# Routing of two mixture-of-experts layers: token table ahead of the pass tables, and one of four place one-hots on ScalarE

## The reference, cut to what matters

```python
def _moe_forward(x, gate_w, wi_gate, wi_up, wo):      # layer 2; N = 2048, E = 8, 512 hidden
    capacity = max(int(N / E * CAPACITY_FACTOR), 1)   # 320
    router_probs = jax.nn.softmax(x_flat @ gate_w.T, axis=-1)
    top_k_probs, top_k_idx = jax.lax.top_k(router_probs, 2)
    top_k_probs = top_k_probs / jnp.sum(top_k_probs, axis=-1, keepdims=True)
    for k in range(2):
        eid = top_k_idx[:, k]
        onehot = (eid[:, None] == experts[None, :]).astype(jnp.int32)
        pos = (cumulative count of onehot)[token, eid] - 1
        disp = zeros(E, capacity, D).at[eid, pos].add(x_flat where pos < capacity)
        expert_out = (silu(disp @ wi_gate) * (disp @ wi_up)) @ wo
        out = out + top_k_probs[:, k] * expert_out[eid, pos]
# layer 3: the same top 2 of 8, without a capacity, h = gelu(x @ w1), out += weight * (h @ w2)
```

## Time and profile before

| | |
|---|---|
| median of 3 runs | 1176.15 us (1174.04 to 1177.28) |
| the profiled execution | 1177.07 us, its span 1175.5 us |
| routing of layer 2, from the router's first product to the first pass | 764.8 to 799.1 us |
| passes of layer 2 | 799.1 to about 909 us |
| routing of layer 3 | 1037.0 to 1071.6 us |
| passes of layer 3 | 1071.6 to about 1150 us |
| busy shares | PE 79%, DVE 72%, ACT 53%, POOL 44% |

### The profile page before, as it was taken

One profiled execution on the slowest core, in us unless ns is written; L12 is line 12 of the kernel. 1 busy time (PEld: TensorE's weight loads), 2 busy tenths in 40 slices (PEclk: granted clock), 3 DMA queues, 4 the chain that ended last, 5 costly groups with the idle time before them and its releaser, 6 DMA issues. The chain is left out here.

```text
span 1175.5 us, 18522 instructions
## 1 busy us (share of the span) xinstructions
PE 928.4 (79%) x5579; PEld 567.1 (48%) x5579; DVE 851.6 (72%) x1652; ACT 626.8 (53%) x1352; POOL 520.9 (44%) x527
## 2 busy tenths in 40 slices
PE   5988799999667856578888888868999296767992
PEld 3523345444445542223223322348999155756982
DVE  6887999999999377878887885184544568985333
ACT  3487798897243443236676667624553393232432
POOL 2056898899501323201111111125653466235773
PEclk9978999999877997669999999858999587867996
DMA  9000000000000301411110010061110200001113
...
DMA packets 28014, 46.29 MB, mean 39 GB/s; under 512 B 8720, under 2 KB 16408, under 8 KB 26896
## 3 DMA queue, kind: packets, MB, share of 16 engines
...
q0 software_dynamic: 4096, 8.35, 2.4%
...
## 5 line engine op out<-in xcount | busy, mean ns | idle before, releaser
L2106 DVE TENSOR_REDUCE sb_l_mxp<-ps 128x2 f32<-128x1024 f32 (+3 forms) x152 | 171.3, 1163 | 40.3 <-PE ps L1919 39.2
L1048 POOL TENSOR_TENSOR sb_gs<-sb_hs,sb_xp 128x512 f32<-128x512 f32 x128 | 162.4, 1296 | 23.9 <-DVE sb_hs L854 12.3
L2049 ACT ACTIVATE sb_l_pT<-ps 128x512 f32<-128x512 f32 (+3 forms) x256 | 111.4, 521 | 75.9 <-PE ps L1974 74.8
L680 PE MATMUL ps<-sb_gs,sb_ident 128*128 128x512 f32 x256 | 131.9, 606 | 0.2
L3042 PE MATMUL ps<-sb_hT,sb_f_shared 128*128 x936 | 121.5, 281 | 1.6 <-ACT sb_hT L3073 1.6
L3042 PEld LDWEIGHTS ps<-sb_hT,sb_f_shared 128*128 128x128 f32 x936 | 113.9, 197 | 2.8 <-issue 2.3
L1974 PE MATMUL ps<-sb_l_qk 51*128 51x512 bf16 (+3 forms) x384 | 88.5, 333 | 18.2 <-ACT sb_l_pT L2049 8.0
L3081 ACT ACTIVATE sb_f_hid<-ps 128x512 f32<-128x512 f32 x78 | 46.6, 597 | 78.6 <-PE ps L3042 78.6
L3140 POOL DMA_INDIRECT moe_y<-sb_f_rows,sb_f_rowi x64 | 64.1, 1001 | 52.9 <-DVE sb_f_rows L3112 41.0
L951 ACT ACTIVATE sb_dA<-sb_dt,sb_negA 128x512 f32<-128x512 f32 x109 | 77.7, 713 | 10.6 <-DVE sb_hs L854 9.8
L3051 PE MATMUL ps<-sb_sw_f_out,sb_f_hid 128*128 x624 | 82.5, 276 | 0.6 <-DVE sb_f_hid L3101 0.6
...
## 6 DMA issues: line engine op xcount, KB each, us to landing
sb_sw_f_in<-w_f_in SPq DMA_DIRECT2D x2, 2048.0 KB, 10.1
...
```

The costliest lines, as they stand in the source:

```text
L680: pe.matmul(ps[:, 4 + e * CPB + hf, :], ident[:], gs[:, p % SL, :], start=False, stop=n == DS - 1).then_inc(acc, 1)
L1048: gp.tensor_tensor(gs[:, q % SL, :], hs[:, q % SL, :], cs[:, k % 2, hf * CH:(hf + 1) * CH], ALU.mult).then_inc(times_c, 1)
L2049: ac.activation(pT[e % 3][:, h, 0:width], ps[:, bank[n_bank], 0:width], ACT.Exp, scale=L2_SCALE).then_inc(exped, 1)
L2106: dv.tensor_reduce(dst, src, AX_X, ALU.max).then_inc(max_out, 1)
```

## The change

Six edits, each in both layers:

1. The one-hots of the experts, `oh`, are written in the order of memory (experts outside, tiles inside), not across it.
2. Two roundings that were an addition and a subtraction in two instructions are one instruction each. The offsets `off` come ahead of `in_blk`, and a second copy of a quarter of them, `off_late`, in 32 bits.
3. VectorE makes three of the four pieces of `at_off`. The fourth (second choice, second half of the tiles) is made by ScalarE: eight Squares of (offset minus index) and one Relu of 1 minus that.
4. `vector_passes` is cut in two. `vector_edges` (the steps on 8 experts) stays behind `at_off`; the rest stands behind `tok_i`. The token table is read with three instructions straight from PSUM.
5. The transposes of chunk 0 back to rows stand behind the ranks with the other three chunks, as do their copies on ScalarE.
6. In the first pass TensorE's transposes of block 1 stand behind the first two of its hidden products.

```diff
@@ -2753,8 +2754,8 @@
             for k in range(2):
-                dv.tensor_tensor(oh[:, k].rearrange("p e t -> p t e"), iota[:].unsqueeze(1).to_broadcast([P, NT, NE]),
-                                 idx[:, :, k].unsqueeze(2).to_broadcast([P, NT, NE]), ALU.is_equal).then_inc(rt_ohb, 1)
+                dv.tensor_tensor(oh[:, k], iota[:].unsqueeze(2).to_broadcast([P, NE, NT]),
+                                 idx[:, :, k].unsqueeze(1).to_broadcast([P, NE, NT]), ALU.is_equal).then_inc(rt_ohb, 1)
             dv.wait_ge(rt_ohb, 3 * nth + 2)
@@ -2799,23 +2800,25 @@
-        def vector_passes():
-            wide = [P, NPASS, NE - 1]
+        def vector_edges():
...
             dv.wait_ge(*v_step.now())
-            dv.tensor_scalar(edge[:], edge[:], ROUND, None, ALU.add).then_inc(*v_step.up())
-            dv.wait_ge(*v_step.now())
-            dv.tensor_scalar(edge[:], edge[:], ROUND, None, ALU.subtract).then_inc(*v_step.up())
+            dv.tensor_scalar(edge[:], edge[:], ROUND, ROUND, ALU.add, ALU.subtract).then_inc(*v_step.up())
             dv.wait_ge(*v_step.now())
...
             dv.tensor_tensor_scan(ends[:], ones[:], ends[:], 0.0, ALU.mult, ALU.add).then_inc(*v_step.up())
-            dv.wait_ge(*v_step.now())
+            at_ends.append(v_step.now())
+        def vector_passes():
+            wide = [P, NPASS, NE - 1]
+            dv.wait_ge(*at_ends[0])
             dv.tensor_tensor(past_end[:], ends[:, 0:NE - 1].unsqueeze(1).to_broadcast(wide),
@@ -2868,48 +2871,51 @@
             dv.wait_ge(*v_step.now())
-            dv.tensor_scalar(sblk[:], sblk[:], ROUND, None, ALU.add).then_inc(*v_step.up())
+            dv.tensor_scalar(sblkb[:], sblk[:], ROUND, ROUND, ALU.add, ALU.subtract).then_inc(*v_step.up())
+            dv.tensor_scalar(sblk[:], sblk[:], ROUND, ROUND, ALU.add, ALU.subtract).then_inc(*v_step.up())
             dv.wait_ge(*v_step.now())
-            dv.tensor_scalar(sblkb[:], sblk[:], ROUND, None, ALU.subtract).then_inc(*v_step.up())
-            dv.tensor_scalar(sblk[:], sblk[:], ROUND, None, ALU.subtract).then_inc(*v_step.up())
-            dv.wait_ge(*v_step.now())
+            dv.scalar_tensor_tensor(off[:], sblk[:], -float(P), slot[:], ALU.mult, ALU.add).then_inc(*v_step.up())
+            at_off_ready = v_step.now()
+            dv.scalar_tensor_tensor(off_late[:], sblk[:, 1, HT:], -float(P), slot[:, 1, HT:], ALU.mult,
+                                    ALU.add).then_inc(rt_at, 1)
             for k in range(2):
...
                                  sblkb[:, k].unsqueeze(2).to_broadcast([P, NT, NSLOT]), ALU.is_equal).then_inc(rt_at, 1)
-            dv.scalar_tensor_tensor(off[:], sblk[:], -float(P), slot[:], ALU.mult, ALU.add).then_inc(*v_step.up())
-            dv.wait_ge(*v_step.now())
+            dv.wait_ge(*at_off_ready)
             for k in range(2):
-                for hf in range(2):
+                for hf in range(2 - k):
                     t0 = hf * HT
...
                                      ALU.is_equal).then_inc(rt_hot, 1)
-            vector_passes()
-            lo, hi = ids[:, 0], ids[:, 1]
+            vector_edges()
+            lo, tables = ids[:, 0], ps[:, 5, 0:2 * NSLOT].rearrange("p (a b) -> p a b", a=2)
+            hi = tables[:, 1]
             dv.wait_ge(rt_mm, r0 + MM_TABLE)
-            dv.tensor_copy(ids[:].rearrange("p a b -> p (a b)"), ps[:, 5, 0:2 * NSLOT]).then_inc(*v_step.up())
-            dv.wait_ge(*v_step.now())
-            dv.scalar_tensor_tensor(lo, lo, float(NT), hi, ALU.mult, ALU.add).then_inc(*v_step.up())
-            at_lo = v_step.now()
+            dv.tensor_copy(lo, tables[:, 0]).then_inc(*v_step.up())
             dv.tensor_scalar(tmp[:], hi, float(NT) + 0.5, float(-NT), ALU.is_gt, ALU.mult).then_inc(*v_step.up())
...
             at_row = v_step.now()
+            dv.wait_ge(*at_tmp)
+            dv.scalar_tensor_tensor(lo, lo, float(NT), hi, ALU.mult, ALU.add).then_inc(*v_step.up())
+            at_lo = v_step.now()
             dv.wait_ge(*at_lo)
             dv.tensor_scalar(tok[:], lo, -1.0, 0.0, ALU.add, ALU.max).then_inc(*v_step.up())
-            dv.wait_ge(*at_tmp)
             dv.wait_ge(*v_step.now())
...
             dv.scalar_tensor_tensor(row[:], tmp[:], float(-(NTOK - NT) // NT), row[:], ALU.mult, ALU.add).then_inc(*v_step.up())
-            dv.wait_ge(*v_step.now())
+            at_row = v_step.now()
+            vector_passes()
+            dv.wait_ge(*at_row)
             dv.scalar_tensor_tensor(row_i[:], lo, -1.0, row[:], ALU.add, ALU.add).then_inc(rt_tables, 1)
...
             for k in range(2):
-                gp.wait_ge(rt_at, 2 * nth + k + 1)
+                gp.wait_ge(rt_at, 3 * nth + k + 2)
                 gp.tensor_tensor(at_blk[:, k, :, 1, :], in_blk[:, k],
@@ -2939,7 +2945,6 @@
             routed(1)
-            back_to_rows(0)
             turned(3)
@@ -2949,13 +2954,16 @@
                       start=True, stop=True).then_inc(rt_mm, 1)
-            for c in range(1, NCH):
+            for c in range(NCH):
                 back_to_rows(c)
             for k in range(2):
-                pe.wait_ge(rt_lo, 2 * nth + k + 1)
+                pe.wait_ge(rt_lo, 3 * nth + k + 1)
                 pe.wait_ge(rt_hi, 2 * nth + k + 1)
                 for hf in range(2):
-                    pe.wait_ge(rt_hot, 4 * nth + 2 * k + hf + 1)
+                    if k + hf < 2:
+                        pe.wait_ge(rt_hot, 3 * nth + 2 * k + hf + 1)
+                    else:
+                        pe.wait_ge(rt_lo, 3 * (nth + 1))
                     for t in range(hf * HT, (hf + 1) * HT):
@@ -2969,16 +2977,20 @@
                 modulate_chunk(l, 1, mod_nth, c)
-                if c == NCH - 2:
-                    rows_evacuated(0)
-            for c in range(1, NCH):
+            for c in range(NCH):
                 rows_evacuated(c)
...
             for k in range(2):
-                ac.wait_ge(rt_at, 2 * nth + k + 1)
+                ac.wait_ge(rt_at, 3 * nth + k + 2)
                 ac.activation(at_blk[:, k, :, 0, :], in_blk[:, k], ACT.Copy, scale=w["c_f2_ids"][:, 2 * NT:2 * NT + 1]).then_inc(rt_lo, 1)
+            apart = hid[:, 0:2, :].rearrange("p z (t n) -> p (z t) n", n=P)
+            for t in range(HT):
+                i = ac.activation(apart[:, t, :], w["c_f2_iota"][:], ACT.Square, scale=-1.0, bias=off_late[:, t:t + 1])
+            i.then_inc(*a_step.up())
+            ac.wait_ge(*a_step.now())
+            ac.activation(at_off[:, 1, HT:, :], apart, ACT.Relu, scale=-1.0, bias=ones[:, 0:1]).then_inc(rt_lo, 1)
@@ -3026,11 +3038,15 @@
         def tensor_step(s):
-            for k in turns(s):
-                gathered(pe, k)
-                past_block(pe, s_x, k - 2)
-                pe.transpose(ps[:, TURN_BANK[k % 2], 0:P], in_q[:, k % QBUF, 0:D], ident[:]).then_inc(s_tr, 1)
+            def turn_blocks():
+                for k in turns(s):
+                    gathered(pe, k)
+                    past_block(pe, s_x, k - 2)
+                    pe.transpose(ps[:, TURN_BANK[k % 2], 0:P], in_q[:, k % QBUF, 0:D], ident[:]).then_inc(s_tr, 1)
             i = s + 1
+            if i != 0:
+                turn_blocks()
             if inside(i):
@@ -3041,6 +3057,8 @@
                                       start=True, stop=True)
+                        if i == 0 and n == 0 and f == FT // 2 - 1:
+                            turn_blocks()
                 m.then_inc(s_up, 1)
```

5 lines of the change are left out of this document (3 added, 2 removed).

## The result

| | before | after |
|---|---|---|
| median | 1176.72 us (1174.04 to 1178.35, 4 runs) | 1162.61 us (1160.65 to 1164.20, 4 runs) |
| ratio | | 0.986, interval 0.982 to 0.990 |
| profiled execution | 1177.07 us | 1160.65 us |

The kernel is 14.1 us faster.

The account below looks back on a forecast made before the run. Passes taken as bound by their start, so time saved in routing reaches the end: 4.6 us in layer 2 plus 4.1 in layer 3, 8.7 in all, median 1167.5 us (chance 0.59), range 1164 to 1171.5.

Parts of the forecast that it names:

- the clock: TensorE's clock around the first passes: 0.5 us lost per layer; bounds 1.9 us gained or 1.8 lost.
- Gelu's table load: Layer 3's first pass: the 1.28 us load ends at T + 8.9, first outputs at T + 10.1, gain 0.45 us.
- Expert one-hots: Routing, both layers: two instructions take 0.6 us in place of 1.23, gain 0.6 us per layer, bounds 0 and 0.9.
- Chunk 0: Its transposes leave the routing chain: 0.7 us gained in layer 3, 0 in layer 2.
- Offsets and GpSimd: Moving `off` ahead of GpSimd's multiplications gains 0.2 us, not 0.85, since the next two-input VectorE instruction waits instead.
- ScalarE's piece: Squares and Relu take 3.7 us, ending before VectorE's third piece in layer 2, after it in layer 3 (1061.3 against 1060.5).
- Rival A: ScalarE's piece comes 1 to 2 us later and bounds; T later by 1.3 us per layer, 1170.1 us; chance 0.17.
- rival B: Rows land too late for the gather, 1.5 us of gain lost; with the clock's bad bound 1171.6 us; chance 0.13.
- Token table: VectorE's reading of it (T) comes 3.1 us sooner in layer 2 and 2.9 in layer 3, before one-hots and transposes.
- T to the passes: From VectorE's token-table reading (T), first pass starts at T + 5.9, before T + 7.5 (layer 2) and T + 6.7 (layer 3).
- C: Passes not bound by their start, GpSimd's turn binds layer 3: gains 0.5 and 2 us, 1173.6 us; chance 0.08.
- D: Slower: TensorE's clock stays at half through the first passes, 25 us more in the two layers; from 1180 us; chance 0.03.

Follow-up runs that it names:

- experiment 3: The changed kernel without the three long products of no use ahead of the passes: 1167.87 us, ratio 0.991 to the kernel before.
- experiment 4: The kernel before with only the long steps of the pass tables moved behind `tok_i`, token table still read by one copy: 1170.13 us, ratio 0.992.
- experiment 9: The kernel before with only the long pass-table steps moved behind `tok_i`, run once more unchanged: 1169.84 us, ratio 0.993.
- experiment 5: The changed kernel with both blocks turned ahead of the first pass, as before the change: 1166.55 us, ratio 0.989 to the kernel before.
- experiment 6: The changed kernel with all four pieces of `at_off` on VectorE, no Squares or Relu on ScalarE: 1163.18 us, ratio 0.987 to the kernel before.

## Why the prediction was wrong

The steps that moved the reading of the token table were right. Of the steps from there on, two terms failed: above all the clock, and in layer 3 the place of Gelu's table load.

- **Expert one-hots**, 0.6 us forecast per layer: 1.23 us became 0.68, 0.55 gained in each. Right. The rule quoted from the Trainium skill (SBUF — State Buffer, the note on cachelines) would have allowed next to nothing; here the measurement decides, and what cost the time was most likely the write across memory. The prediction said that the read of `idx` in steps of 32 bytes stays. In fact it became more frequent: the old order stood still on one value of `idx` for eight elements, the new one steps at each element, and the two are faster all the same. The read of `iota` went the other way, from stepping to standing still, and no run changed the write alone.
- **Chunk 0**, 0.7 us in layer 3: 0.46 in one profile, 0.87 in the other, and no difference in the timed runs. Right in size, partly given back.
- **Offsets and GpSimd.** `off` went from 1.03 to 0.19 us, and two of the three pieces of `at_off` now take 2.07 us, where before it was one of four: the wait moved to the next long instruction, as I had reckoned. The instructions of that line, both layers, with ns min/median/max:

```profile
L2888 DVE TENSOR_TENSOR sb_f_shared<-sb_sc_f_iota,sb_f_soff x6: 1210/2066/2069, 777.0 to 1047.2; 128x1024 bf16<-128x1024 bf16 x6
```

  The trace agrees with the exclusion that the Trainium skill states (SBUF — State Buffer, "Who interferes with whom"), for which the sum had 0.2 us in place of 0.85: GpSimd's first multiplication takes 1.36 us, and its second, which runs into VectorE's pieces, 1.91 (2.13 before).
- **ScalarE's piece.** Eight Squares 2.43 us and the Relu 1.15, 3.58 together against a forecast of 3.7. First in layer 2, last in layer 3 by 0.64 us (forecast 0.8). Rival A fell.
- **Token table**, 3.1 and 2.9 us from the count to T: 3.18 and 3.05. Right.
- **T to the passes**, forecast T + 5.9 in both layers: T + 5.88 and T + 5.48. Pass tables and weights were covered: `x_at` was there at T + 3.6 (786.91), forecast T + 3.4. The rows landed 6.5 to 6.8 us after issue, the last at 782.80, ahead of the first gather at 785.17, so that rival B fell.
- **The clock** is the step that failed most. The prediction said "where it rises now I can't say", gave bounds of 1.9 us gained and 1.8 lost per layer, and took 0.5 lost in each. From the start of the passes to the first outputs the measured gain is 1.43 us in layer 2 (5.33 to 3.90) where the sum had 0.75 lost, and 0.61 in layer 3 (3.79 to 3.18) where T to the first outputs was to gain 0.45 less 0.5 and gained 1.87. These terms are off by 2.2 and 1.9 us, 4.1 together, and 3.1 of it is the clock (the rest is the next point). The clock stayed at 2.4 GHz from the long products on in both layers, and experiment 3, in which it didn't, has the first outputs 2.6 and 0.9 us later. 8.7 and 4.1 make 12.8 us, and the parts measured 12.2; GpSimd's turn took 0.4 to 0.8 back in layer 3.
- **Gelu's table load in layer 3** was mis-sized. The sum let it end at T + 8.9 and put the first outputs at T + 10.1. By its own rows it ended at T + 8.0 before (1071.50 and 1.28, less 1064.81), and it was measured at T + 7.9 (1056.35 and 1.28, less 1049.72). These 1.0 us have nothing to do with the clock. What held the first outputs before was TensorE at half clock, busy without a gap from 1071.55 until they started at 1075.34.
- **The shorter idle stretch could have been worked out, the clock could not.** Before, the long products started behind the last product at 789.1 and ended at 793.4 (796.69 less 3.29), 4.3 us. In the new order they start at T less 0.2 us and end at T + 4.1, and my own step put the first block's transpose at T + 5.1. So the idle stretch had to shrink from 3.3 us to 1 or less. I had counted the new order's effect on every engine but not on this stretch, although I had written that the clock falls in it. But 1 us is just the size at which it fell twice (experiments 4 and 9) and once did not (experiment 5). That the changed kernel kept it in both layers of the two profiles is in part luck: in three of these four stretches the clock rose so late that the long products took 4.9 to 5.1 us and filled the stretch by themselves.
- **The range** was too narrow by its own terms: with the good bound of the clock in both layers the sum gives 13.5 us, 1162.6 us, and I let it end at 1164.0. The bound was in the prediction and not in the range.

Rivals C and D didn't come about. C's mechanism is there in small: GpSimd's turn in layer 3 is longer by 0.4 to 0.8 us after an earlier start.

No experiment beats the changed kernel by more than the intervals: those with all pieces on VectorE and with chunk 0 first are its equals. Of the change's six edits, edit 4 carries most, 4.0 us up to T in the two layers. By the profiles edit 6 is worth 0.9 us, edit 3's ScalarE piece 1.3 up to T, edit 5 about 0.5. Edit 1 was not undone in any run; by the length of its instructions it is worth 1.1. Edit 2 and the shorter reading of the token table were not tried by themselves either; from the count to T, experiments 4 and 6, which differ there in these and in edit 5, lie 0.45 and 0.5 us apart. The clock belongs to none of them alone: with edit 4 alone it fell in layer 2 in both profiles, and without edit 6 it stayed up in one.
